# Projections in row halves, in two phases, in the attention of layer two of a four-layer network

## The reference

```python
def _L1_attn_ref(x, qkv, out_w, rpe_bias):      # 16 heads of 64
    q, k, v = jnp.einsum('bsx,xMnd->Mbnsd', x, qkv)
    a = jnp.einsum('bnsd,bntd->bnst', q, k) * q.shape[-1] ** (-0.5)
    cum = jnp.cumsum(rpe_bias[:, :s], axis=-1)
    rel = jnp.arange(s)[:, None] - jnp.arange(s)[None, :]
    bias = jnp.where(rel >= 0, cum[:, jnp.clip(rel, 0)], PAD)
    a = jax.nn.softmax(a + bias, axis=-1)
    mix = jnp.einsum('bnst,bntd->bnsd', a, v)
    return jnp.einsum('bnsd,ndx->bsx', mix, out_w)
...
x = x + _L1_attn_ref(xn, ...) + _L1_ffn_ref(xn, ...)
```

## Time and profile before

| | us |
|---|---|
| median of 3 runs | 2346.9 (2346.76 to 2347.49) |
| the profiled execution | 2347.72 |
| its span, first to last instruction | 2345.9 |
| TensorE busy in the span | 2102.0, 90% |
| VectorE, ScalarE, GpSimd busy | 1630.3, 1325.4, 945.8 |
| attention of layer two, groups 0 and 1 (`a_`) | from 133 to 397 |
| attention of layer two, groups 2 to 7 (`a1b_`) | from 549 to 1299 |

### The profile page before, as it was taken

One profiled execution on the slowest core, in us unless ns is written; L12 is line 12 of the kernel. 1 busy time (PEld: TensorE's weight loads), 2 busy tenths in 40 slices (PEclk: granted clock), 3 DMA queues, 4 the chain that ended last, 5 costly groups with the idle time before them and its releaser, 6 DMA issues. The chain is left out here.

```text
span 2345.9 us, 51161 instructions
## 1 busy us (share of the span) xinstructions
PE 2102.0 (90%) x19252; PEld 1298.8 (55%) x19252; DVE 1630.3 (69%) x4801; ACT 1325.4 (56%) x2688; POOL 945.8 (40%) x1175
## 2 busy tenths in 40 slices
PE   4679998998999999999999796899999985899886
PEld 2447776996677777777776665233333334333333
DVE  7666663775666676666665553999989946589896
ACT  2247775655777777777777242276767672323322
POOL 2036765664668734665343032111111110054462
PEclk9689998999999999999999698699999996899998
DMA  6311112214011100000000053111211101000000
GB/s 178 109 59 37 37 36 70 68 37 147 20 35 20 35 2 20 2 20 2 2 2 2 13 177 117 30 40 40 49 37 37 37 7 37 0 0 0 9 9 18
DMA packets 77908, 93.78 MB, mean 40 GB/s; under 512 B 10145, under 2 KB 56242, under 8 KB 76002
## 3 DMA queue, kind: packets, MB, share of 16 engines
q1 hardware_dynamic: 64178, 77.23, 11.0%
q0 software_dynamic: 13488, 13.28, 2.8%
HBM read 54.55 MB, written 35.53 MB: 38 GB/s over the span
## 5 line engine op out<-in xcount | busy, mean ns | idle before, releaser
L1069 ACT ACTIVATE WA<-a_E 128x1024 f32<-128x1024 f32 (+1 forms) x320 | 282.8, 939 | 128.2 <-PE a_E L1002 70.2
L982 PE MATMUL a_S<-a_KS,a_QS 54*128 54x512 bf16 (+3 forms) x768 | 202.3, 354 | 37.4 <-DVE a_mx L1104 26.4
L455 POOL TENSOR_SCALAR WA<-WA,a1b_rinv 128x1024 f32<-128x1024 f32 (+3 forms) x192 | 147.8, 818 | 159.5 <-DVE a1b_rinv L754 159.4
L455 POOL TENSOR_SCALAR XR<-XR,a1b_rinv 128x768 f32<-128x768 f32 (+3 forms) x192 | 145.1, 784 | 155.9 <-DVE a1b_rinv L754 155.6
L572 PE MATMUL a1b_O<-a1b_PT,WA 128*64 128x128 f32 x3072 | 188.9, 276 | 0.0
L572 PEld LDWEIGHTS a1b_O<-a1b_PT,WA 128*64 128x64 f32 x3072 | 165.8, 137 | 6.5
L982 PEld LDWEIGHTS a_S<-a_KS,a_QS 54*128 54x128 bf16 x768 | 53.5, 94 | 205.0 <-DVE a_mx L1104 102.1
L1020 PE MATMUL a_O<-WA,V 128*9 128x512 f32 (+3 forms) x1536 | 159.9, 504 | 0.1
L1102 DVE TENSOR_REDUCE a_mx<-a_S 128x1 f32<-128x512 f32 x256 | 156.8, 681 | 1.7 <-PE a_S L982 1.7
L535 PE MATMUL a1b_B<-a1b_Kf,a1b_Qf 64*128 64x512 f32 (+2 forms) x768 | 153.4, 471 | 1.3 <-DVE a1b_firstmax L741 1.1
L670 ACT ACTIVATE WA<-WA,a1b_nmax 128x1024 f32<-128x1024 f32 (+3 forms) x192 | 150.3, 787 | 1.3 <-DVE a1b_nmax L741 1.3
(11 more groups left out here) (497 smaller groups left out, 5400.6 us busy)
## 6 DMA issues: line engine op xcount, KB each, us to landing
WA<-in_w SPq DMA_DIRECT2D x8, 1024.0 KB, 9.0
a_QS<-qstack SPq DMA_DIRECT2D x32, 216.0 KB
a_KS<-kstack SPq DMA_DIRECT2D x32, 216.0 KB
a1b_tb<-tab SPq DMA_DIRECT2D x12, 512.0 KB, 4.7
qstack<-f_parts SPq DMA_DIRECT2D x24, 256.0 KB, 3.8
kstack<-f_parts SPq DMA_DIRECT2D x24, 256.0 KB, 3.9
f_slots<-f1r_zrows SPq DMA_DIRECT2D x9, 516.0 KB
f1t_xs<-f_slots SPq DMA_DIRECT2D x9, 516.0 KB, 7.2
```

The costliest lines, as they stand in the source:

```text
L455: pool.tensor_scalar(v, v, rinv[:, e, u, part:part + 1], 1.0, ALU.mult, ALU.mult).then_inc(n_sb, 1)
L982: ins = pe.matmul(pS[(at + half) % SB][:, lo:lo + n], QS[s][ROW[half], pair, i * P:(i + 1) * P], KS[s][ROW[half], pair, c * CH:c * CH + n] ...
L1069: act.activation(PT[q % NP][:, :, 0:w], pE[q % 2][:, :, 0:w], ACT.Exp).then_inc(e_sb, 1)
```

## The change

In each step the two projections are cut into the array's row halves. `project_rows` and `output_rows` make a 128 x 128 block from 64 of the 128 rows. `beside` issues them in two phases: in the first, bank P gets its rows 0 to 63 and bank C1 its rows 64 to 127, in the second the other way round, added to what is there. Phase one stands before `scores(step + 2, 2)`, phase two behind `turn(step, 2)`. The new semaphore `pc_ps` makes phase two wait for phase one's last matmuls. `turn(step, 2)` writes to columns 256 to 383 of banks B0 and B1, which are now one tensor, `pair`, and VectorE alone copies it out, both halves in one instruction (`copy_last`). `scores` waits once for both heads. On VectorE the second `inverse` now precedes the last copy and the last two biases.

```diff
-    BY_ACT, BY_DVE = 4, 2
+    BY_ACT, BY_DVE = 3, 2
...
-    pA, pB, pC = ([ph.ps(f"{n}{h}") for h in range(2)] for n in "ABC")
+    pA, pC = ([ph.ps(f"{n}{h}") for h in range(2)] for n in "AC")
+    pair = ph.ps("B", (P, HG, CH))
+    pB = [pair[:, h, :] for h in range(2)]
     pS = (pB, pA, pB)
-    pT = (pA, pC, pC)
+    pT = (pA, pC, [bank[:, 2 * P:3 * P] for bank in pB])
...
+            def project_rows(bank, p, kind, half, t, k, order):
+                rows, b = slice(k * QH, (k + 1) * QH), p % B
+                out, i = bank[:, t * P:(t + 1) * P], half * CT + t
+                xnt = XNT[rows, b, 1 + i * P:1 + (i + 1) * P]
+                lhs, rhs = (xnt, wv[rows, :]) if kind == 2 else ((wq, wk)[kind][rows, :], xnt)
+                ins = pe.matmul(out, lhs, rhs, start=order + t == 0, stop=order + t == CT)
+                if t == CT - 1 and order == 1:
+                    ins.then_inc((q_ps, k_ps, v_ps)[kind], 1)
+                return ins
...
+            def beside(it, e, order):
+                step = it * E + e
+                if order:
+                    pe.wait_ge(pc_ps, begun[step + 1])
+                for t in range(CT):
+                    last_p, last_c = None, None
+                    if e == 0 and it + 1 < IT:
+                        last_p = project_rows(pP, it + 1, 0, 1, t, order, order)
+                        last_c = project_rows(pC[1], it + 1, 1, 0, t, 1 - order, order)
+                    elif e == 1 and it + 1 < IT:
+                        last_p = project_rows(pP, it + 1, 1, 1, t, order, order)
+                        last_c = project_rows(pC[1], it + 1, 2, 0, t, 1 - order, order)
...
+                    for ins in (last_p, last_c):
+                        if ins and order == 0 and t == CT - 1:
+                            ins.then_inc(pc_ps, 1)
...
+                if n == 0 and step:
+                    pe.wait_ge(s_sb, step * R)
+                    if step > 2:
+                        pe.wait_ge(t_sb_a, (step - 2) * BY_ACT)
+                        pe.wait_ge(t_sb_d, (step - 2) * BY_DVE)
...
                 for u in range(HG):
                     head = slice(u * D, (u + 1) * D)
-                    if n == 0 and step:
-                        pe.wait_ge(s_sb, step * R - 1 + u)
...
                     scores(step + 2, 1)
-                    scores(step + 2, 2)
-                    turn(step, 2)
+                    pe.wait_ge(t_sb_a, step * BY_ACT + 3)
...
+                    beside(it, e, 0)
+                    scores(step + 2, 2)
+                    turn(step, 2)
+                    beside(it, e, 1)
...
                     exponential(step + 1, 0, 1)
-                    copy(step, 2)
                     exponential(step + 1, 1, 1)
...
+            def copy_last(step):
+                dve.wait_ge(t_ps, step * 3 + 3)
+                dve.tensor_copy(turned_last[step % 2].rearrange("p (j h q) -> p h j q", h=2, q=QH),
+                                pair[:, :, 2 * P:3 * P].rearrange("p h (j q) -> p h j q", q=QH)).then_inc(t_sb_d, 1)
...
                     inverse(step + 1, 0)
-                    bias(step + 2, order[1], 0)
-                    copy(step, 2)
-                    bias(step + 2, order[1], 1)
+                    for u in range(HG):
+                        bias(step + 2, order[1], u)
+                    inverse(step + 1, 1)
+                    copy_last(step)
                     for u in range(HG):
                         bias(step + 2, order[2], u)
-                    inverse(step + 1, 1)
```

More of the change, by code:

```diff
@@ L391, in attention @@
         ph.sem(n) for n in ("tps", "tsba", "tsbd", "pvps", "osb", "yps", "xsb"))
+    pc_ps = ph.sem("pcps")
+    begun = [0]
+    for it in range(IT):
+        for n in range(E):
+            begun.append(begun[-1] + (2 * (it + 1 < IT), 2 * (it + 1 < IT),
+                                      (it + 1 < IT) + (it > 0), (it > 0) + (it + 2 < IT))[n])
     def tile_of(e, c):
@@ L502, in project, with output_rows @@
                     ins.then_inc(v_ps, 1)
-            def output(bank, p, j):
-                if p < 0:
-                    return
-                if p % B == 0 and j == 0:
-                    pe.wait_ge(wo_ok, p // B + 1)
-                pe.wait_ge(o_sb, p * 2 + j + 2)
+            def project_rows(bank, p, kind, half, t, k, order):
[7 more added lines that the diff above has]
+                return ins
+            def output_rows(bank, p, j, t, k, order):
+                rows, i = slice(k * QH, (k + 1) * QH), TILES[j][t]
+                ins = pe.matmul(bank[:, t * P:(t + 1) * P], mU[p % 2][rows, i * P:(i + 1) * P], wo[rows, :],
+                                start=order + t == 0, stop=order + t == CT)
+                if t == CT - 1 and order == 1:
+                    ins.then_inc(y_ps, 1)
+                return ins
+            def output(bank, p, j):
                 for t, i in enumerate(TILES[j]):
@@ L544, in turn @@
                     pe.wait_ge(t_sb_d, (step - 1) * BY_DVE + 1)
-                elif r == 2:
-                    pe.wait_ge(t_sb_a, step * BY_ACT + 3)
-                elif step:
-                    pe.wait_ge(t_sb_a, step * BY_ACT)
+                elif r == 2 and step + 2 >= ALL:
+                    pe.wait_ge(s_sb, ALL * R)
                     pe.wait_ge(t_sb_d, step * BY_DVE)
@@ L743, in bias, with copy_first @@
                                          scalar=least, op0=ALU.add, op1=ALU.min, accum_out=peak).then_inc(s_sb, 1)
-            def copy(step, r):
-                dve.wait_ge(t_ps, step * 3 + r + 1)
-                dve.tensor_copy(*half(step, r, 1)).then_inc(t_sb_d, 1)
+            def copy_first(step):
+                dve.wait_ge(t_ps, step * 3 + 1)
+                dve.tensor_copy(*half(step, 0, 1)).then_inc(t_sb_d, 1)
+            def copy_last(step):
+                dve.wait_ge(t_ps, step * 3 + 3)
+                dve.tensor_copy(turned_last[step % 2].rearrange("p (j h q) -> p h j q", h=2, q=QH),
+                                pair[:, :, 2 * P:3 * P].rearrange("p h (j q) -> p h j q", q=QH)).then_inc(t_sb_d, 1)
             def inverse(step, u):
@@ L780, in _ @@
                     order = wide_first((step + 2) % E)
-                    copy(step, 0)
+                    copy_first(step)
                     for u in range(HG):
```

66 lines of the change are left out of this document (34 added, 32 removed).

## The result

| kernel | median of the runs shown, lowest to highest (us) | ratio to before, 95% interval | profiled run's span (us) |
|---|---|---|---|
| before | 2347.2 | | 2345.9 |
| changed | 2325.6 (2321.5 to 2328.1) | 0.9902 (0.9883 to 0.9921) | 2326.2 |

The forecast was 2314 with a range of 2299 to 2332. The time lies inside that wide range, but outside the forecast's own one of 2307 to 2322, and only two thirds of the forecast gain arrived: 21.6 us for 33. The profiled execution took 2328.06 us.

What follows compares the result with a forecast made beforehand. TensorE's own order of work was taken as the bound. Per iteration of 30.53 us: 1.37 - 0.23 + 0.38 - 0.29 - 0.07 = 1.16; 27.5 iterations 31.9, with ends 33; 2346.9 - 33 = 2314, own range 2307 to 2322, wide 2299 to 2332.

Steps and rivals of the forecast that it cites:

- mode changes gone, less phase two's late weights: TensorE around the projections: full-array/half-array gaps of 0.34 us a step go, 1.37 an iteration; phase two behind transposes pays 0.23.
- earlier second reciprocal: VectorE: GpSimd's scaling ends 0.4 us earlier or more, so TensorE's stalls before second turns go, 0.38 an iteration.
- wait for Q, first step: Second turns wait for bank C until VectorE copies Q out: 0.23 us, and 0.06 for halves out of step.
- first scores behind VectorE's last biases, second step: With a first maximum, first scores wait for both heads' last biases: 0.07 us in one step of four.
- the last one on the new waits: ScalarE empties K and V one behind the other, the second out before its bank is wanted: nothing, within 0.1.
- Slots: One 128-column pass in each row half, 16 a step, taken at 0.11 us each: nothing gained, nothing lost.
- The third rival: Weight loads show in every projection slot: 2519 us, slower from 0.126 a slot on; chance 0.06.
- the fourth rival: The 0.34 a step belongs to taking up new operands behind waits, not the mode: 2347 to 2350 us; chance 0.05.
- The two terms that it names: What the own range rests on: slots from 0.108 to 0.113 us, and the Q wait from 0.1 to 0.5.
- The first rival: VectorE's copy, last biases and addition crowd behind turn 2: an iteration loses 0.45, 12 us back, 2326 us; chance 0.16.
- The wait between the phases: Phase two's wait for phase one's last matmuls is over before it is reached, by 0.1 us or so.
- The lone projections: At the stretches' ends, 8 steps with one projection only: +0.5 us each, about half hidden by waits, 2 us lost.

Runs made afterwards that it cites:

- the reciprocal alone: The kernel before with only VectorE's second reciprocal moved ahead of the last two biases: 2324.3 us, ratio 0.9894.
- the copy split: The kernel with both waits gone, its wide copy out of pair B split between ScalarE and VectorE, whose last biases wait for ScalarE's copy: 2298.8 us, ratio 0.9794.
- the full-array experiment: The changed kernel with both phases in their places but made of full-array matmuls, one whole projection each: 2372.0 us, ratio 1.0095.
- both waits gone: The changed kernel with first scores waiting for K's first half alone and VectorE emptying Q before it adds to X: 2303.1 us, ratio 0.9809.
- both phases late: The kernel with both waits gone, with phase one moved behind the last scores and turn 2, directly ahead of phase two: 2341.9 us, ratio 0.9985.

## Why the prediction was right or wrong, point by point

| term, us an iteration | forecast | measured | by |
|---|---|---|---|
| mode changes gone, less phase two's late weights | +1.14 | +1.07 | 30.07 with the reciprocal alone, 29.0 for four undisturbed steps |
| earlier second reciprocal | +0.38 | +0.47 | 30.54 to 30.07 |
| wait for Q, first step | -0.29 | -0.27 | 7.52 to 7.25 |
| first scores behind VectorE's last biases, second step | -0.07 | -0.10 | 7.35 against 7.25 |
| first scores behind K, third step | 0 | -0.41 | 7.70 to 7.29 |
| the rest of the third step | 0 | -0.04 | 7.29 to 7.25 with the copy split |
| sum | 1.16 | 0.72 | 29.82 |

**The step that failed** is the last one on the new waits: "Where K and V are emptied by ScalarE one behind the other, the second is out at about S + 1.3, in front of S + 1.42. Nothing, within 0.1." (S is the start of the next step, its turn 0.) The time of the copies was right: V leaves at 934.14 + 0.59 = S + 1.27. But only the next use of the banks was followed. K's own reader was not: the first scores two steps ahead stand at S + 0.49 and want K, which is in memory at S + 0.78. It costs 0.41 in one step of four, 10.9 us. For Q both had been asked, for K one.

**Slots.** 0.11 through all 16 and 0.16 for the first behind transposes: as forecast. By the rule of the Trainium skill that stood against the change (TensorE: Matmul & The Clock Gate, Part 3, "The mechanism") each slot would have shown a load. In this trace slot behind slot in the same row halves stood 0.11 apart, each with weights of its own, so the measurement decides against it here. The third rival, which needed 0.126, falls.

**Mode changes.** The 0.34 a step was right in size (0.35 for the same pair in the full-array experiment), and it is the mode: the fourth rival falls.

**The reciprocal.** The mechanism was right, the size half: the kernel with this edit alone is 19.5 us faster by spans and 24 by medians, where 0.38 x 27.5 = 10.5 had been counted. The sum read two late steps of an iteration where there are three, and gave the ends nothing for it; first and last steps, with stalls of up to 1.38 behind GpSimd in the kernel before, gave 6.2 us more. With 14.7 + 6.2 = 20.9 for 10.5 this term is off by 10 us, about as much as the missing K term takes away. So the sum came nearer than its terms, and that is luck: two errors of 10 to 11 us of opposite sign. Its own range of 2307 to 2322 missed even so. The two terms that it names reach further than it says, to 2314 + 2048 x 0.003 + 27.5 x 0.27 = 2327, and neither of them is what went wrong.

**VectorE's tail.** The copy out of pair B takes 0.40 to 0.43, forecast 0.42. In two steps of four it delays nobody; splitting it gave back 0.04 in each of the others. The first rival, which would have given 2326, named the right time for a wrong reason: its price of 0.1 in three steps and 0.15 in one is not in the trace.

**The wait between the phases** was free in its place, as forecast. The estimate behind it (met 0.17 after the slot) was too short: back to back it cost 0.35, against the 0.34 that lie between the phases.

**Left out:** the square root. TensorE wants the turned copies earlier and ScalarE gets to its 2 x 1.28 + 0.32 later, so they are no longer covered: 2.4 us lost in the profiled execution, of which about 1 is the low clock (the step took 9.45 for 10.50 where the clock stayed).

**The ends.** The lone projections were counted at -2 and the ends' full steps at +3, 1 gained. Against the kernel with the reciprocal alone the changed one loses 5.3 there (151.2 for 145.9), 4.8 of it in the two last steps. Some 2.7 of that belong to this execution: in the first stretch TensorE waits 0.85 ahead of phase two, and the values behind it take 3.4 for 1.8 at a granted clock of 0.76. With both waits gone (2303.1) the two last steps took 10.3 each, still 1.6 above the kernel before, where a lone projection has two phases instead of one and 0.78 is waited for ScalarE ahead of the last outputs. The cost of a lone projection was in the sum, that wait was not.

## What to carry to other kernels

When a producer moves later in a step, list every reader of its result, not only the next user of its bank, and ask of each reader which part it needs: a wait for a whole tensor, where half is read, was free until its end moved by a microsecond, and then cost 11 us, half of what the whole change gained. Run each part of a change alone before believing the sum: here the smallest edit, one instruction moved up by two places, was worth as much in the old kernel as the whole change, and the large part (the projections) was worth nothing until two waits of its own making were taken away, and then 21 us (2324.3 to 2303.1). Count the ends of a pipeline separately, since a step with less work in it shows lateness that the steady steps cover: here they gained 6.2 us by one part of the change and lost 5.3 by the other.

## What the runs showed of the hardware that was not expected

- A wait between two groups of half-array passes on TensorE's own queue, for results of the first group, costs 0.25 over the slot of 0.11, and the first slot behind it another 0.10 (both phases late: 981.10, 981.47, 981.69). The 0.34 of other work between the phases hid it whole.
- Two heads' matmuls in the two row halves that are released apart didn't gain: 0.04 less in the scores, 0.05 more in the turns behind.
- The same stall of 1.92 us of TensorE was followed by a granted clock of 0.53 to 0.68 over 3.6 us in three kernels and of 1.00 in three others whose queues differ elsewhere. A fall costs about 1 us there and 1.6 in a last step but one.
- Entering and leaving full-array mode between two groups of scores cost 0.43, between transposes 0.35.
